# A selective scan in four sweeps: zero-weight matrix products beside y's halves on TensorE, and the scan's bodies written out instead of looped

## The reference

```
def step(hst, ins):
    dt_t, B_t, C_t, x_t = ins
    dA = jnp.exp(dt_t[:, :, None] * A)
    hst = hst * dA + (dt_t * x_t)[:, :, None] * B_t[:, None, :]
    y_t = jnp.einsum('bds,bs->bd', hst, C_t)
    return (hst, y_t)
```

## Time and profile before

| | |
|---|---|
| median of 3 runs | 7390.89 us (7389.54 to 7392.94) |
| the profiled execution | 7387.62 us |
| its span, first to last instruction | 7385.8 us |
| the scan's steps | from 934 to 5026 us of the span |
| mean granted TensorE clock, whole span | 0.701 |

### The profile page before, as it was taken

The page is one execution under the profiler, slowest core; times in us unless marked ns, Lnnn a source line. Parts: engine busy times, 40 slices in busy tenths (PEclk is TensorE's granted clock), DMA queues, the critical chain, the costliest instruction groups (busy, mean ns, idle before and its releaser), DMA issues. The chain is left out here.

```text
span 7385.8 us, 182682 instructions
## 1 busy us (share of the span) xinstructions
PE 6787.5 (92%) x68920; PEld 3195.0 (43%) x68920; DVE 4254.5 (58%) x6974; ACT 4687.8 (63%) x9618; POOL 3328.7 (45%) x2814
## 2 busy tenths in 40 slices
PE   6888599999999999999999999997989999979888
PEld 3444344444444444444444444443444544535444
DVE  2555466666666666666666666664443543545554
ACT  3555477777777777778777788772234534435554
POOL 0101166666666666666666666661022322323333
PEclk8999755555555555555555555557999999989999
DMA  5555512121212212211122112215410000000000
GB/s 185 157 145 146 142 53 54 53 56 54 61 53 56 55 54 59 56 54 54 54 56 62 54 55 55 55 50 193 143 46 6 10 9 6 7 33 10 13 12 6
DMA packets 596322, 458.63 MB, mean 62 GB/s; under 512 B 449728, under 2 KB 504640, under 8 KB 577280
## 3 DMA queue, kind: packets, MB, share of 16 engines
q1 hardware_dynamic: 594624, 445.32, 20.8%
q10 hardware_dynamic: 832, 1.57, 0.1%
HBM read 301.29 MB, written 145.49 MB: 60 GB/s over the span
## 5 line engine op out<-in xcount | busy, mean ns | idle before, releaser
L1444 POOL TENSOR_TENSOR s_dec<-s_hs,s_dec 128x512 f32<-128x512 f32 x2040 | 2553.2, 1276 | 1467.0 <-DVE s_hs L1484 890.8
L1374 ACT ACTIVATE s_dec<-s_pa 128x512 f32<-128x512 f32 x4096 | 2236.7, 602 | 95.2 <-PE s_pa L1249 38.7
L1286 PE MATMUL s_py<-s_hs,s_cz 128*32 128x256 f32 x16384 | 2183.6, 630 | 0.0
L1473 DVE TENSOR_TENSOR s_pA<-s_pA,s_dec 128x512 f32<-128x512 f32 x2040 | 1397.5, 696 | 965.0 <-ACT s_hs L1380 639.8
L1380 ACT COPY s_hs<-s_pA 128x512 f32<-128x512 f32 x2048 | 1218.7, 595 | 711.5 <-PE s_pA L1259 710.7
L1249 PE MATMUL s_pa<-s_dl,s_al 18*128 18x64 bf16 x32768 | 1545.8, 235 | 88.6 <-DMA s_dl<-D 48.6
L1484 DVE TENSOR_TENSOR s_hs<-s_pB,s_dec 128x512 f32<-128x512 f32 x2040 | 1324.8, 686 | 401.6 <-PE s_py L1286 311.9
L1259 PE MATMUL s_pA<-az 18*128 18x256 bf16 x4096 | 1194.1, 399 | 77.4 <-DVE s_pA L1473 71.4
L1249 PEld LDWEIGHTS s_pa<-s_dl,s_al 18*128 18x128 bf16 x32768 | 1172.8, 120 | 182.6 <-issue 57.6
L1259 PE MATMUL s_pB<-az 18*128 18x256 bf16 x4096 | 1225.6, 399 | 19.9 <-DVE s_hs L1484 19.9
L1259 PEld LDWEIGHTS s_pB<-az 18*128 18x128 bf16 x4096 | 261.9, 102 | 1583.5 <-issue 862.8
(11 more groups left out here) (254 smaller groups left out, 5966.6 us busy)
## 6 DMA issues: line engine op xcount, KB each, us to landing
s_dl<-D SPq DMA_DIRECT2D x512, 144.0 KB
az<-U SPq DMA_DIRECT2D x1024, 72.0 KB
az<-B SPq DMA_DIRECT2D x1024, 36.0 KB
D<-p_dp SPq DMA_DIRECT2D x64, 384.0 KB, 5.8
U<-p_up SPq DMA_DIRECT2D x60, 384.0 KB, 6.1
B<-p_bz SPq DMA_DIRECT2D x144, 128.0 KB, 2.5
SZ<-p_sz SPq DMA_DIRECT2D x16, 1024.0 KB, 4.0
SK<-p_skip SPq DMA_DIRECT2D x16, 1024.0 KB, 5.8
```

The source lines that it names most:

```text
L1286: mm = pe.matmul(py[QR * k:QR * (k + 1), HALF * v:HALF * (v + 1)], cz[:, 2 * k + v, at:at + QR], hs[k][:, x % 2, HALF * v:HALF * (v + 1)], ...
L1374: act.activation(dec[w][:].rearrange("p k i t d -> p (k i t) d")[:, :, DS * q + d:DS * q + d + 8], pa[:, bank, :].rearrange("p (d c) -> p ...
L1444: pool.tensor_tensor(m, two(hs[k][:, (x + 1) % 2, :]), m, ALU.mult).then_inc(m_done, 1)
L1473: dve.tensor_tensor(state, state, of_chunk(k, x), ALU.mult).then_inc(mul, 1)
```

## The change

A tile `still` in bf16 holds 512 columns of ones and 32 columns of zeros. A helper `keep_warm` issues two rounds of four products: the weights are the zeros (128 partitions x 32 columns), the moving operand the ones (128 x 512), and the output adds 0 to y's bank `s_py`, at the same four column groups as y. It is called right after y's half v=0 and right after the half v=1, in each step but these: in step x=1 neither call is made, in x=0 the one after v=1 is not, and at the very start there is no y to stand beside. That gives 28 calls in body 0 and 29 in each of the other 63, 1855 calls of 8 products. Nothing waits for them, and they wait for nothing of their own.

`bodies` no longer uses a hardware loop: it emits all 64 bodies one after the other, with constant semaphore values.

```diff
+        still = sb("still", [P, W + QR], BF16)
...
-        def bodies(eng, body):
-
-            made = 2 * T - 2
-            body(0, 0, True, False, True, None)
-            with eng.Fori(0, SWEEPS - 1) as i:
-                for q in range(1, BODIES + 1):
-                    body(BODIES * i + q, made * i + 2 * (BODY * q - q // BODIES), q == BODIES, False, False,
-                         64 * i + 128 if q == BODIES - 1 else None)
-            for q in range(1, BODIES):
-                body(ALL - BODIES + q, made * (SWEEPS - 1) + 2 * BODY * q, False, q == BODIES - 1, False, None)
+        def bodies(body):
+
+            for G in range(ALL):
+                sweep, g = G // BODIES, G % BODIES
+                turn = g == BODIES - 1 and G < ALL - 1
+                body(G, 2 * (BODY * G - sweep), g == 0, G == ALL - 1, G == 0, 64 * (sweep + 2) if turn else None)
...
+                def keep_warm():
+
+                    for _ in range(2):
+                        for k in range(CH):
+                            pe.matmul(py[QR * k:QR * (k + 1), :], still[:, W:W + QR], still[:, 0:W],
+                                      start=False, stop=False, skip_group_check=True)
...
                             y(n - 1, before, 0)
+                            keep_warm()
...
                         if has and not late:
                             y(n - 1, before, 1)
+                            if x:
+                                keep_warm()
...
                 pool.memset(ident[:], 0.0).then_inc(zeroed, 1)
-                pool.wait_ge(zeroed, 3)
+                pool.memset(still[:, 0:W], 1.0).then_inc(zeroed, 1)
+                pool.memset(still[:, W:W + QR], 0.0).then_inc(zeroed, 1)
+                pool.wait_ge(zeroed, 5)
```

More of the change, by code:

```diff
@@ L1362, in _ @@
                         to_b(0, 0, 0, k, v)
-                bodies(pe, body)
+                bodies(body)
                 y(BODY * ALL - 1, BODY - 1, 0)
@@ L1420, in _ @@
                         take(p, p, e, (2 * p + e) % BANKS, 0)
-                bodies(act, body)
+                bodies(body)
                 p = 15 + 33 * (ALL - 1) + 17
@@ L1462, in _ @@
                 fill(0)
-                bodies(pool, body)
+                bodies(body)
             @block.vector
@@ L1502, in body @@
                             plus(n, made, x, k, start)
-                bodies(dve, body)
+                bodies(body)
                 take_y(ALL)
```

## The result

The changed kernel takes 7130.25 us (median of 4 runs, 7129.15 to 7152.74) against 7391.85 us before: the ratio is 0.9655, 95% interval 0.9638 to 0.9671. It is faster by 262 us. Forecast were 546 us, so the direction and the rise of the clock came, and less than half of the size.

The account below looks back on a forecast made before the run. PE was taken to bound the low-clock scan, ACT the high-clock step. A body of 16 x 3.08 + 3.5 + 2.6 = 55.4 us made the scan 3546 against 4092, giving 6845 us; range 6620 to 7100, chance 0.73.

Parts of the forecast that it names:

- The bound and the way to the gain: In the scan, PE bounds the low-clock step (3.74 us); calls with y's 128-partition footprint raise the clock and mostly keep it up.
- the clock stays low: Rival: zero weights do not raise the scan's clock, and 1855 calls cost 0.86 us each on PE: 8970 us, chance 0.08.
- The prices of a call and of a plain step: In the scan, a call costs 0.44 us high, 0.86 low; a step with calls 3.08 us high, 5.45 low.
- Time at the low level that is left: Per scan body, 6 us assumed still at the low clock, losing 2.6 us; bounds none and 12 us (5.2 lost).
- what a body costs beyond its steps: Per scan body, 3.5 us at the high level on top of 16 steps, mostly the decay buffer's change at x=0 and x=8.
- Both dips: Low-clock places expected in a body: the decay buffer's change, and step x=1 without y or calls; 6 us low assumed.
- the swing: Rival: dips at x=0, 1 and 8 drop the scan's clock; about 7150 us at low share 0.3, chance 0.14.
- The loop's turns: Three turns of the scan's hardware loop, where PE stands on issue, cost 17 us that writing out removes.
- the waits' register instructions: Register instructions of the waits in the looped bodies, priced at nothing.
- The calls in series: Rival: a call's eight products run one after another, 1.76 us a call, 5.6 a step, 9290 us; chance 0.03.
- a lack of instructions: Rival: instructions come too late in straight code, 4 us a step at the high level, 7620 us; chance 0.02.

## Why the prediction was right or wrong

**The bound and the way to the gain were right.** The scan did run at the low level with PE busy, and the calls raised it. The run with 32 partitions bears out that this takes y's footprint in partitions and not PE's being busy. The rival *the clock stays low* describes that run: its 8970 us stands beside 9002 measured.

**The prices of a call and of a plain step were right.** A call is 0.43 us (taken 0.44), the high step 3.02 (3.08), the low step 5.44 (5.45). One reading under them is loose: two `bu` starting 0.19 us apart are not quite 256 columns at 1.2 GHz, which take 0.21; the sum used the latter.

**The step that failed is "Time at the low level that is left".** The prediction assumed 6 us a body, bounded by none and 12. Measured are 17.4. In the kernel with only the buffer change filled (the fill itself cost nothing, and the other calls are the same) a body that passes wholly at the high level lasts 53.6 us; the changed kernel's mean is 59.8. So the low time costs 6.2 us a body where the sum had 2.6, and 3.6 x 64 = 230 us were left out.

**A second term was too small.** For "what a body costs beyond its steps" the prediction took 3.5 us; it is 53.6 - 16 x 3.02 = 5.3, another 1.8 x 64 = 115 us. The prediction put most of its 3.5 down to the change of the buffer. That is some 3 us; steps x=1 and x=2, which it did not name, are some 2 more. Here is x=2, from copy to copy, in the kernel with both gaps filled, at the high level:

```profile
2036.98 0.59 ACT L1401 COPY s_hs<-s_pA 128x512 f32<-128x512 f32 x1 [1.01 <-PE s_pA L1256]
...
2040.47 0.77 ACT L1415 COPY s_ys<-s_pa 128x128 f32<-128x128 f32 x4 [0.45 <-PE s_pa L1310]
2041.29 0.59 ACT L1401 COPY s_hs<-s_pA 128x512 f32<-128x512 f32 x1
```

It lasts 4.31 us, 1.3 more than a plain step: in x=2 PE turns the taken y, and ACT waits for that and copies it. With both terms and the smaller high step (16 x 0.06 x 64 = 61 us less) the forecast would have been 6845 + 230 + 115 - 61 = 7129, beside 7130. It has to close so well, since the terms are read from the changed kernel's own body of 59.8 us; what is separate evidence is the 53.6.

Two things were wrong in the low time. Both dips were seen, but no row gave what either does to the clock. At the standstill before x=0 it came down in all 63 bodies, the step without y kept it down or brought it down again in 40, and filling both takes away nearly all low time. And the way back was thought short, because the one rise in the earlier trace rows came soon after a dense piece of work; the clock now stays low for up to 24 us at a stretch, beside the very calls that hold it once it is high, as in the row of 17 us at 0.51 with PE busy 99%. The upper bound of 12 us had no row behind it.

**The rival that came true is the swing.** At a share of 0.3 it gave a step of 3.54 us and about 7150. The Trainium skill ("TensorE: Matmul & The Clock Gate", on PSUM-queue depth-cycling) describes such a pattern, a clock that swings because of short waits between groups of products. This trace agrees for the wait before x=0, with a fall in 63 of 63 bodies, and filling that wait took all of them away; for the fall at x=1 the wait alone is not the cause, as the run with both gaps filled shows. The rival had been given 0.14.

**Smaller points.** The loop's turns were priced 17 us and the waits' register instructions at nothing, and writing out is worth 32 alone, 11 with the clock held; in the changed kernel itself it went with a loss of 42 against the looped one. The calls in series and a lack of instructions were excluded by the rows above: 72 products and their loads in 3.02 us.

What stays open: what makes the spells behind x=0 now 3 and now 24 us long was only seen, not taken apart. Nor is it known why the same standstill of 1.03 us brings the clock down at x=0 in all 63 bodies and at x=8 in only 10 (43 with the calls at x=0 and x=1). And that the register waits are what makes a looped body 0.31 us longer was only argued.

## What to carry to other kernels

Where PE is busy and the clock low, look at how many partitions its products fill: here filler of 128 partitions beside them raised the clock, and filler of 32 partitions brought nothing and cost 1612 us. Put it first where PE stands still; about a microsecond of waiting that recurs was worth more here (198 us) than the steps left out (63), and both together 327. When the clock is held, cut the filler down until the next engine's step is the length. Judge such a change by the time that remains at the low level in each period, since there the filler itself costs twice as much (0.86 us a call instead of 0.43).

## What the runs showed that was not expected

- Zero weights against a tile of ones are enough to raise and hold the clock: 0.99 over the scan with both gaps filled. Other values in their place were not tried.
- Where the clock keeps falling, small shifts in time hide other edits: the same calls in a loop gave 7088 us and written out 7130, though writing out gains 32 us by itself.
- A third call on the path at the buffer change (0.43 us, twice a body) cost nothing measurable, 6798 against 6804 us.
